# Down products with the tokens on the partitions in both feed-forwards, GpSimd's low part of v behind the router, and ten idle products ahead of the gates

## The reference

```
x = x + L0_xattn(layernorm(x), ctx, ctx, ...)   # mLSTM cell with 4 heads over the context
x = x + L0_ffn(layernorm(x), ...)               # 16 experts of width 64, top 4 by sigmoid score, and a shared one
x = x + L1_xattn(layernorm(x), ctx, ctx, ...)   # softmax attention with 16 heads
x = x + L1_ffn(layernorm(x), ...)               # 8 experts of width 512, top 2 by softmax

# L0_ffn, for every expert:
    h = silu(x @ gate_e.T) * (x @ up_e.T)
    y = y + c_e[:, None] * (h @ w2_e.T)         # c_e: the gate of each token, 0 where not chosen
# L1_ffn, for every expert:
    h = gelu(x @ w1_e.T)
    out = out + comb[:, e:e+1] * (h @ w2_e.T)
```

## Time and profile before

| | us |
|---|---|
| median of 3 runs | 310.8 (310.58 to 314.33) |
| the profiled execution's own time | 312.89 |
| its span, first to last instruction | 310.9 |
| TensorE busy | 236.2 |
| VectorE busy | 232.5 |
| ScalarE busy | 173.4 |
| GpSimd busy | 173.4 |
| mean granted TensorE clock | 0.919 |

### The profile page before, as it was taken

The page is one execution under the profiler, slowest core; times in us unless marked ns, Lnnn a source line. Parts: engine busy times, 40 slices in busy tenths (PEclk is TensorE's granted clock), DMA queues, the critical chain, the costliest instruction groups (busy, mean ns, idle before and its releaser), DMA issues. The chain is left out here.

```text
span 310.9 us, 4815 instructions
## 1 busy us (share of the span) xinstructions
PE 236.2 (76%) x1428; PEld 120.0 (39%) x1428; DVE 232.5 (75%) x477; ACT 173.4 (56%) x308; POOL 173.4 (56%) x172
## 2 busy tenths in 40 slices
PE   8499874591889797755648358695979999999982
PEld 3235661261233332333537356352423333333431
DVE  4928579887689778679898856555677978879672
ACT  1041334160666566338887733456868788788870
POOL 2959093675288894178435410202488967868331
PEclk9969996956699999999996959979999999999998
DMA  7701400010011004003000000000021021000002
GB/s 268 290 0 36 102 2 0 0 50 0 2 45 34 25 25 135 0 0 133 4 2 3 0 1 2 0 2 1 0 69 64 6 67 67 0 0 2 1 0 67
DMA packets 6788, 11.73 MB, mean 38 GB/s; under 512 B 1136, under 2 KB 4336, under 8 KB 6640
## 3 DMA queue, kind: packets, MB, share of 16 engines
q1 hardware_dynamic: 5664, 10.61, 10.7%
q10 hardware_dynamic: 1104, 0.87, 0.9%
HBM read 9.91 MB, written 0.52 MB: 34 GB/s over the span
## 5 line engine op out<-in xcount | busy, mean ns | idle before, releaser
L1024 DVE SCALAR_TENSOR_TENSOR attention_or_experts<-attention_or_experts 128x512 f16<-128x512 f32 x64 | 63.7, 1011 | 22.2 <-ACT attention_or_experts L646 22.1
L634 ACT ACTIVATE attention_or_experts<-ps 128x512 f32<-128x512 f32 x64 | 38.2, 597 | 16.5 <-PE ps L1341 15.6
L435 POOL TENSOR_TENSOR attention_or_experts<-attention_or_experts 128x512 f32<-128x512 f32 x16 | 25.4, 1590 | 33.0 <-DVE attention_or_experts L1032 21.3
L646 ACT ACTIVATE attention_or_experts<-attention_or_experts 128x512 f16<-128x512 f32 x64 | 40.1, 629 | 0.0
L326 POOL TENSOR_TENSOR rstd<-ve,minus_half 128x4 f32<-128x4 f32 x8 | 8.2, 1024 | 45.3 <-DVE ve L689 45.3
L1350 PE MATMUL ps<-attention_or_experts,wsp 128*128 128x512 f16 x64 | 24.7, 386 | 8.1 <-DVE attention_or_experts L1024 4.9
L1065 PE MATMUL ps<-idle 128*128 128x512 f16 x90 | 24.5, 431 | 8.0 <-ACT v L509 6.0
L426 POOL TENSOR_TENSOR attention_or_experts<-attention_or_experts 128x1024 f16<-128x1024 f32 x8 | 17.0, 2129 | 16.0 <-ACT attention_or_experts L598 16.0
L1341 PE MATMUL ps<-xhi,wsp 128*128 128x512 f16 x64 | 24.5, 383 | 0.0
L1340 PE MATMUL ps<-xlo,wsp 128*128 128x512 f16 x64 | 24.5, 383 | 0.0
L1339 PE MATMUL ps<-xhi,wsp 128*128 128x512 f16 x64 | 24.5, 383 | 0.0
(11 more groups left out here) (205 smaller groups left out, 605.9 us busy)
## 6 DMA issues: line engine op xcount, KB each, us to landing
raw<-w_second SPq DMA_DIRECT2D x8, 512.0 KB, 3.6
raw<-w_first SPq DMA_DIRECT2D x9, 192.0 KB, 2.3
attention_or_experts<-ctx_v SPq DMA_DIRECT2D x1, 1056.0 KB, 9.1
rw<-rows ACTq DMA_DIRECT2D x1, 512.0 KB, 6.2
ctxT<-ctx_t SPq DMA_DIRECT2D x1, 512.0 KB, 6.5
kS<-xhi SPq DMA_DIRECT2D x8, 64.0 KB, 2.0
kS<-xlo SPq DMA_DIRECT2D x8, 64.0 KB, 2.0
out<-xr SPq DMA_DIRECT2D x2, 256.0 KB, 2.5
```

The source lines that it names most:

```text
L435: pool.tensor_tensor(yT[:, g, :], yT[:, g, :], ytmp[:, g, :], ALU.add).then_inc(s["yacc"], 1)
L634: a.activation(h32[:, k % 4, :], bank(k % 4), ACT.Gelu, scale=1 / (XS * XS)).then_inc(s["gelu"], 1)
L646: a.activation(hhi[:, k % 4, :], h32[:, k % 4, :], ACT.Copy, scale=HS).then_inc(s["hhi1"], 1)
L1024: v.scalar_tensor_tensor(hlo[:, k % 4, :], h32[:, k % 4, :], HS, hhi[:, k % 4, :], ALU.mult, ALU.subtract)\
```

## The change

- In both feed-forwards the down products swap their operands: h (high or low, 128 tokens) is loaded as the weights and the down weights (128 columns) are streamed. Each group of three matmuls of 512 columns becomes 4 x 3 of 128 columns. The result has the tokens on the partitions.
- FFN0's end: no scaled copy, no transposes; VectorE adds bank 6+g, scaled, to xr in one operation.
- FFN1: no broadcast of gates, no `combT`, no gate transposes and copies; the gates stay in `gate1` per token, and for each tile VectorE does one scalar_tensor_tensor that multiplies the bank by the token's gate and adds xr. `ytmp`, `yT`, GpSimd's `accumulate`, the final transposes and the last add go; the output's DMAs wait for these sums.
- `sel1` and its DMA go.
- GpSimd's v1lo waits for `comb_ready`, the end of the first router.
- Ten idle products (`keep_warm(4, 10)`) stand between the first up products and the gates' transposes.

```diff
+        gate1 = sb("gate1", [P, G, TG, X1])
-        yT = work(1, [P, G, N])
-        ytmp = work(1, [P, 2, N])
-            sp.dma_start(sel1[:], sel_second).then_inc(s["in_sel"], 16)
             for g in range(G):
-                sp.wait_ge(s["x_out"], g + 1)
+                sp.wait_ge(s["yacc"], 2 * X1 - 1 + g)
                 sp.dma_start(out_v[:, gt(g), :], xr[:, gt(g), :]).then_inc(s["out_done"], 16)
...
             pool.wait_ge(s["v1hi_ready"], 1)
+            pool.wait_ge(s["comb_ready"], G)
             pool.tensor_tensor(v1lo[:], v1[:], v1hi[:], ALU.subtract).then_inc(s["v1lo_ready"], 1)
...
-            def accumulate(n, g):
-                pool.wait_ge(s["ymul"], n + 1)
-                pool.wait_ge(s["yacc"], n)
-                pool.tensor_tensor(yT[:, g, :], yT[:, g, :], ytmp[:, g, :], ALU.add).then_inc(s["yacc"], 1)
-            pool.wait_ge(s["yTp"], G)
-            pool.memset(yT[:], 0.0).then_inc(s["acc_zero"], 1)
...
-            for g in range(G):
-                a.wait_ge(s["mm2"], reached(2 * PAIRS - 1 + g))
-                a.activation(yT[:, g, :], bank(6 + g), ACT.Copy, scale=1 / (XS * HS)).then_inc(s["yT_ready"], 1)
...
+            def add_y(g):
+                v.wait_ge(s["mm2"], reached(2 * PAIRS - 1 + g))
+                stat(v.scalar_tensor_tensor(xr[:, gt(g), :], bank(6 + g).rearrange("p (t e) -> p t e", e=E), 1 / (XS * HS),
+                                            xr[:, gt(g), :], ALU.mult, ALU.add))
...
-                route(v.scalar_tensor_tensor(r[:, 5], r[:, 1], 1.0, r[:, 4], ALU.add, ALU.mult))
-                route(v.tensor_copy(combt[:, g, :, 0:X1], r[:, 5]))
-                v.tensor_tensor(combt[:, g, :, 32:32 + X1], r[:, 5], combt[:, g, :, 0:X1], ALU.subtract)\
-                    .then_inc(s["comb_ready"], 1)
+                v.scalar_tensor_tensor(gate1[:, g], r[:, 1], 1.0, r[:, 4], ALU.add, ALU.mult).then_inc(s["gate1_ready"], 1)
...
-                v.tensor_tensor(ytmp[:, g, :], bank(4 + g), cb[:, g, :], ALU.mult).then_inc(s["ymul"], 1)
+            def add_expert(n, q, g, e):
+                v.wait_ge(s["mm2b"], n + 1)
+                v.wait_ge(s["gate1_ready"], g + 1)
+                v.wait_ge(s["yacc"], reached(q))
+                for t in range(TG):
+                    c = gate1[:, g, t, e:e + 1] if type(e) is int else gate1[:, g, t, bass.ds(e, 1)]
+                    x_t = xr[:, g * TG + t, :]
+                    last = v.scalar_tensor_tensor(x_t, bank(4 + g)[:, t * P:(t + 1) * P], c, x_t, ALU.mult, ALU.add)
+                last.then_inc(s["yacc"], 1)
...
-                mm(bank(6 + k), wsp[:, p, 0, c], hhi[:, k, :], start=first, stop=False)
-                mm(bank(6 + k), wsp[:, p, 0, c], hlo[:, k, :], start=False, stop=False)
-                mm(bank(6 + k), wsp[:, p, 1, c], hhi[:, k, :], start=False, stop=last).then_inc(s["mm2"], 1)
+                for t in range(TG):
+                    ts = slice(t * P, (t + 1) * P)
+                    o = bank(6 + k)[:, ts]
+                    mm(o, hhi[:, k, ts], wsp[:, p, 0, c], start=(first and t == 0), stop=False, skip_group_check=True)
+                    mm(o, hhi[:, k, ts], wsp[:, p, 1, c], start=False, stop=False, skip_group_check=True)
+                    done = mm(o, hlo[:, k, ts], wsp[:, p, 0, c], start=False, stop=last, skip_group_check=True)
+                done.then_inc(s["mm2"], 1)
...
                 inner0(g, 0, g, 0)
+            keep_warm(4, 10)
             for g in range(G):
                 transpose_gates(0, g)
...
-                if c == 0:
-                    pe.wait_ge(s["cbx1"], before(q, first))
-                    pick = sel1[:, e + p, :] if type(e) is int else sel1[:, bass.ds(e + p, 1), :].rearrange("p a m -> p (a m)")
-                    mm(bank(6 + g), pick, combT[:, g, :], start=True, stop=True)
...
                 if c == 0:
-                    pe.wait_ge(s["ymul"], before(q, first))
-                mm(bank(4 + g), wsp[:, p, 0, cs], hhi[:, k % 4, :], start=(c == 0), stop=False)
-                mm(bank(4 + g), wsp[:, p, 0, cs], hlo[:, k % 4, :], start=False, stop=False)
-                mm(bank(4 + g), wsp[:, p, 1, cs], hhi[:, k % 4, :], start=False, stop=(c == FC - 1)).then_inc(s["mm2b"], 1)
+                    pe.wait_ge(s["yacc"], before(q, first))
+                for t in range(TG):
+                    ts = slice(t * P, (t + 1) * P)
+                    o = bank(4 + g)[:, ts]
+                    mm(o, hhi[:, k % 4, ts], wsp[:, p, 0, cs], start=(c == 0 and t == 0), stop=False, skip_group_check=True)
+                    mm(o, hhi[:, k % 4, ts], wsp[:, p, 1, cs], start=False, stop=False, skip_group_check=True)
+                    last = mm(o, hlo[:, k % 4, ts], wsp[:, p, 0, cs], start=False, stop=(c == FC - 1), skip_group_check=True)
+                last.then_inc(s["mm2b"], 1)
...
                 if i == NT + 1:
                     keep_warm(3, 16)
-                    transpose_gates(1, 0)
...
-            pe.wait_ge(s["yacc"], 2 * X1)
-            for g in range(G):
-                transpose_y(g, g, s["yTp1"])
```

80 lines of the change are left out of this document (20 added, 60 removed).

## The result

The median of four executions is 298.1 us (297.97 to 300.28), against 310.7 (310.52 to 314.33) before: a ratio of 0.9585, with a 95% interval of 0.950 to 0.967, and 12.6 us less. The profiled execution took 298.2 us with a span of 296.4; before it was 312.9 and 310.9.

A forecast was written before the change was run, and what follows sets the result against it. No engine was taken to bound the kernel throughout; in the second feed-forward TensorE sets the pace, VectorE where GpSimd runs beside it. The terms summed to -16.0 us, from 310.8 to 294.8 us, with an 8 in 10 range of 289 to 301.

The follow-up runs named there:

- pool_sums: The changed kernel with GpSimd's sixteen 128x512 sums put back on spare tiles that nothing reads: 302.8 us, ratio 0.968 to the kernel before.
- split_pool: The changed kernel with VectorE's four adds per expert in two halves, placed later, and GpSimd's sixteen spare sums put back: 296.4 us, ratio 0.954 to the kernel before.

## What to carry to other kernels

Where a gate is per token, let the output of the down projection have the tokens on the partitions: four 128-column products with their loads cost what one of 512 columns does, and gate and residual go into one operation that reads PSUM, free from GpSimd's holds. When an operation is moved on GpSimd, look at once for the operation with two SBUF inputs that it holds in its new place; the hold moves along, it doesn't vanish, and is worth moving to where the busiest engine has slack (3.7 us became 0.3 here). And a block of work on a helper engine costs by where it stands: before counting its busy time, look at what the busiest engine waits for behind it, and try it later and in pieces.

## What the hardware showed that had not been expected

- The lower clock level wanders. Ahead of the router, in work that is the same in all kernels, the max search came between 64.9 and 68.4 us, by where and how long the slow stretches fell; in the attention's first part it makes up to 3 us. A difference of 2 us between two single profiles, in stages that an edit doesn't touch, says nothing of the edit.
- At the lower level, down products start 0.107 us apart, for 0.056 at the full one: the short products scale with the clock as the long ones do (0.43 and 0.216). The timeline of TensorE, start of FFN1 in the kernel after, at a granted clock of 0.5:

```profile
197.37 0.31 PE L1307 MATMUL ps<-wsp,attention_or_experts 128*128 128x128 f16 x1
197.48 0.31 PE L1308 MATMUL ps<-wsp,attention_or_experts 128*128 128x128 f16 x1
197.58 0.31 PE L1309 MATMUL ps<-wsp,attention_or_experts 128*128 128x128 f16 x1
```

- Four adds of 128x128 from PSUM, each with a pointer scalar, take 1.13 us. The mean of one is 0.34 to 0.345 us in all profiles of the new kernels, with GpSimd's sums beside them (pool_sums, split_pool) and without.
